# An attention stage that makes the next stage's weight parts in place, with outputs' parts and fetched sums a pair behind

## The reference, cut to what matters

```python
q = _l2norm(q)                      # (B, 16, 1024, 64)
k = _l2norm(k) * key_temp           # (B, 4, 1024, 64), repeated 4 times
scores = jnp.einsum('bhqd,bhkd->bhqk', q, kg) * scale
attn = jax.nn.softmax(jnp.where(causal, scores, min), axis=-1)
out = jnp.einsum('bhqk,bhkd->bhqd', attn, vg)
return out.transpose(0, 2, 1, 3).reshape(B, S, LATENT) @ w_o.T
...
x = x + s * g                       # end of layer 0
xn = _layernorm(x, axis=-1)         # layer 1 begins
q, k, v = xn @ wq.T, xn @ wk.T, xn @ wv.T
low = jnp.einsum('bsd,hrd->bshr', x, A)
```

## Time and profile before

| | us |
|---|---|
| median of three runs | 2434.13 |
| profiled execution, its own time | 2439.68 |
| its span in the profile | 2437.6 |
| attention stage, first exp to last (L2145) | 1048.8 to 1439.4 |
| busy over the whole span: PE, DVE, ACT, POOL | 2036.1, 1523.0, 1127.0, 818.7 |
| mean granted clock of TensorE | 0.928 of 2.4 GHz |

### The profile page before, as it was taken

One profiled execution on the slowest core, in us unless ns is written; L12 is line 12 of the kernel. 1 busy time (PEld: TensorE's weight loads), 2 busy tenths in 40 slices (PEclk: granted clock), 3 DMA queues, 4 the chain that ended last, 5 costly groups with the idle time before them and its releaser, 6 DMA issues. The chain is left out here.

```text
span 2437.6 us, 47417 instructions
## 1 busy us (share of the span) xinstructions
PE 2036.1 (84%) x19400; PEld 995.0 (41%) x19400; DVE 1523.0 (62%) x3033; ACT 1127.0 (46%) x2021; POOL 818.7 (34%) x782
## 2 busy tenths in 40 slices
PE   7999989997578899867878859776488988888878
PEld 3444435554233334533444424333244443444434
DVE  3543354434679998435766663556788888888813
ACT  1221146554323342155655630233277777777760
POOL 0210312122545646222565320224443334334310
PEclk9999999998789999888989979988699999999999
DMA  6020101103222112453312338322664564543424
GB/s 233 35 87 35 67 16 31 31 14 118 78 62 80 50 52 69 142 138 57 105 66 83 118 104 217 101 74 74 131 148 67 70 85 65 74 79 58 68 72 145
DMA packets 162028, 207.08 MB, mean 85 GB/s; under 512 B 58962, under 2 KB 100436, under 8 KB 159124
## 3 DMA queue, kind: packets, MB, share of 16 engines
q1 hardware_dynamic: 158756, 189.83, 31.7%
q10 hardware_dynamic: 3056, 14.23, 1.7%
HBM read 139.75 MB, written 64.25 MB: 84 GB/s over the span
## 5 line engine op out<-in xcount | busy, mean ns | idle before, releaser
L3278 DVE TENSOR_REDUCE f_chunk_max<-f_ps_a 128x64 f32<-128x1024 f32 x320 | 319.4, 1032 | 47.5 <-PE f_ps_a L3022 25.0
L3151 ACT ACTIVATE conv_in<-f_ps_s 128x512 f32<-128x512 f32 x480 | 258.7, 603 | 86.9 <-PE f_ps_s L3053 42.3
L2145 ACT ACTIVATE d_probs<-d_ps_s,d_shift 128x512 f32<-128x512 f32 (+3 forms) x384 | 194.2, 589 | 92.1 <-PE d_ps_s L2061 66.6
L3022 PE MATMUL f_ps_a<-conv_in 128*32 128x512 bf16 (+3 forms) x3072 | 201.4, 340 | 41.1 <-DVE f_chunk_max L3278 24.3
L3053 PE MATMUL f_ps_s<-f_qs,f_ks 128*32 128x512 bf16 x2304 | 209.3, 384 | 23.2 <-ACT f_qs L3142 14.6
L2056 PE MATMUL d_ps_s<-conv_in 128*64 128x512 f16 (+3 forms) x768 | 137.4, 360 | 76.9 <-ACT d_probs L2145 68.0
L1422 PE MATMUL c_ps_c<-conv_in,c_wT 128*128 128x512 f16 x768 | 184.9, 400 | 18.0 <-DVE c_odd L1723 13.6
L3218 POOL TENSOR_SCALAR f_absent<-f_rest 128x576 f32<-128x576 f32 x32 | 54.4, 1699 | 304.1 <-DVE f_rest L3295 180.1
L2072 PE MATMUL d_ps_o<-d_probs,conv_in 128*64 128x512 f32 (+3 forms) x768 | 150.3, 500 | 5.3 <-ACT d_probs L2145 4.4
L3075 PE MATMUL f_ps_o<-conv_in,f_v 128*32 128x512 f32 (+2 forms) x1152 | 125.6, 522 | 27.4 <-ACT conv_in L3151 27.4
L3142 ACT ACTIVATE f_qs<-f_ps_s 32x512 bf16<-32x512 f32 x192 | 112.6, 586 | 75.7 <-PE f_ps_s L3036 73.2
(11 more groups left out here) (379 smaller groups left out, 4539.1 us busy)
## 6 DMA issues: line engine op xcount, KB each, us to landing
conv_in<-qk SPq DMA_DIRECT2D x96, 128.0 KB, 4.1
f_qs<-qk SPq DMA_DIRECT2D x96, 128.0 KB, 4.7
conv_in<-q_parts SPq DMA_DIRECT2D x8, 1024.0 KB, 5.2
o_parts<-d_o_part SPq DMA_DIRECT2D x32, 256.0 KB, 2.3
conv_in<-o_parts SPq DMA_DIRECT2D x8, 1024.0 KB, 8.4
qk<-e_part SPq DMA_DIRECT2D x12, 640.0 KB, 4.9
f_qs<-qk SPq DMA_DIRECT2D x96, 64.0 KB, 4.6
rows<-in_qc_w ACTq DMA_DIRECT2D x3, 1536.0 KB, 7.0
```

Of the source, the lines that this page charges most:

```text
L2145: act.activation(probs[n % RING][SCORES[c][1]][:, lo:hi], ps_s[c % BANKS][:, lo - hi + CH:], ACT.Exp, bias=shift[:, 0:1], scale=HD0 ** -0. ...
L3022: last = pe.matmul(out[side(e), h, 0:w], qa[u][:, 2 * p + h, side(e, qt * P)], ka[u][:, kh * CH:kh * CH + w], start=True, stop=not last_keys)
L3151: act.activation(probs[m % HELD][:, :, at:at + P], bank_of["s", i, n][:].rearrange("p (h n) -> p h n", n=P), ACT.Exp, scale=HD1 ** -0.5).t ...
L3278: dve.tensor_reduce(chunk_max[:, qt - 2, :, at:at + w // CHUNK], src.rearrange("p h (c k) -> p h c k", k=CHUNK), AX.X, ALU.max).then_inc(a ...
```

## The change

Three things in the attention stage change, and with them the layout of the next stage's weights.

1. *Outputs' parts a pair later.* ACT makes `high(p-2)` after kt 2 of pair p, where it made `high(p-1)` after kt 6. DVE makes `low(p-2)` after the third gather, just ahead of `divide(p-1)`, where it stood ahead of `combine(p-1)`. After the last pair ACT makes two of them.
2. *Fetched sums later.* The fetches come after steps 7 and 24 instead of 4 and 19; `sizes` go to pairs 1 and 3, `scales` to pairs 2 and 4 and ahead of the combine, and the pieces to pairs 5 to 12.
3. *Parts in place.* POOL writes the scaled fp32 piece to a small buffer `w_scaled` in `d_w_space`, and both fp16 parts over the piece itself, which has just their size. The stores to `e_parts`, the load back and POOL's waits for the stores are gone. The parts of a piece now lie behind each other in `whole`, so the middle stage addresses them piece by piece.

```diff
-        SPLIT_FROM, SPLIT_EACH = 4, 2
+        SPLIT_FROM, SPLIT_EACH = 5, 2
...
-                if SPLIT_FROM < p <= LAST_SPLIT + 1:
-                    store_pieces(p - 1)
...
-                if p == LAST_SPLIT + 1:
-                    for i in range(2):
-                        sp.wait_ge(split_stored[i], 16 * ((len(PIECES) + 1 - i) // 2))
-                    weights.load_parts(sp)
...
-                if kt == 6 and p > 0:
-                    high(p - 1)
+                if kt == 2 and p > 1:
+                    high(p - 2)
...
-                elif n == 4:
+                elif n == 7:
                     fetch(0, 1, 0)
...
-                elif n == QT + SIZES + 2:
+                elif n == QT + SIZES + 7:
                     fetch(1, SIZES, 1)
             copy(ALL - 1)
+            high(ALL - 2)
             high(ALL - 1)
...
-                to, src = w_parts[x % 2], weights.whole[:, at:at + n]
+                src, whole = w_scaled[x % 2][:, 0:n], weights.whole[:, at:at + n]
+                to = whole.bitcast(FP16).rearrange("p (a c) -> p a c", a=2)
                 pool.wait_ge(scaled, 4)
                 if x >= 2:
-                    pool.wait_ge(split_stored[x % 2], 16 * (x // 2))
-                pool.tensor_scalar(src, src, weights.scale[:, own:own + 1], None, ALU.mult).then_inc(split, 1)
+                    pool.wait_ge(split, 3 * (x - 1))
+                pool.tensor_scalar(src, whole, weights.scale[:, own:own + 1], None, ALU.mult).then_inc(split, 1)
...
-                if p > 1:
-                    low(p - 2)
+                if p in (2, SPLIT_FROM - 1):
+                    scales(*((0, 1, 0) if p == 2 else (1, 4, 1)))
                 if p > 0:
                     combine(p - 1)
                 gather(p, 2)
-                if p == 0:
+                if p > 1:
+                    low(p - 2)
+                if p == 1:
                     sizes(0, 1, 0)
-                elif p == 2:
+                elif p == 3:
                     sizes(1, 4, 1)
...
-        self.oT = [x.rearrange("p (m d) -> p m d", d=D) for x in oT]
+        self.oT = oT.rearrange("p (m a d) -> p a m d", a=2, d=D)
```

More of the change, by code:

```diff
@@ L1931, in attend_phase @@
         root = sb("root", [P, 4])
-        w_parts = [w_space[:].bitcast(FP16)[:, n * 2 * (CH + 16):(n + 1) * 2 * (CH + 16)].rearrange("p (a c) -> p a c", a=2) for n in range(2)]
+        w_scaled = [w_space[:, n * (CH + 16):(n + 1) * (CH + 16)] for n in range(2)]
         temp = sb("temp", [P, 1])
@@ L1963, in attend_phase @@
         split = sem("d_split")
-        split_stored = [sem(f"d_split_stored{i}") for i in range(2)]
         o_high = sem("d_o_high")
@@ L1994, in store @@
                     sp.dma_start(dram["o0_parts"][n, g * (G0 // 2) + i, :, b * S:(b + 1) * S], o_parts[p % 2][n][:]).then_inc(stored[p % 2], 16)
[L1996 to L2000, removed]
             sp.dma_start(v_w[:].rearrange("p (k c) -> p k c", k=KD), dram["w_qkvT"].rearrange("p (k o) -> p k o", k=KD)[:, :, LAT + KVD:LAT + 2 * KVD])\
@@ L2286, in _ @@
                 gather(p, 2)
-                if p == 0:
+                if p > 1:
+                    low(p - 2)
+                if p == 1:
                     sizes(0, 1, 0)
-                elif p == 2:
+                elif p == 3:
                     sizes(1, 4, 1)
-                elif p in (1, SPLIT_FROM - 1):
-                    scales(*((0, 1, 0) if p == 1 else (1, 4, 1)))
                 if p > 0:
@@ L2326, in __init__ @@
         self.ends = [sum(self.WIDTHS[:i]) for i in range(len(self.WIDTHS) + 1)]
-        self.parts = self.whole[:].bitcast(FP16).rearrange("p (a n) -> p a n", a=2)
-        oT, qkT, tokT = [[self.parts[:, part, lo:hi] for part in range(2)] for lo, hi in zip(self.ends, self.ends[1:])]
-        self.oT = [x.rearrange("p (m d) -> p m d", d=D) for x in oT]
-        self.qkT = [x.rearrange("p (i k n) -> p i k n", i=self.NQK, k=KD) for x in qkT]
-        self.tokT = [x.rearrange("p (k t) -> p k t", k=KD) for x in tokT]
+        oT, qkT, tokT = [self.whole[:, lo:hi].bitcast(FP16) for lo, hi in zip(self.ends, self.ends[1:])]
+        self.oT = oT.rearrange("p (m a d) -> p a m d", a=2, d=D)
+        self.qkT = qkT.rearrange("p (i a k n) -> p a i k n", i=self.NQK, a=2, k=KD)
+        self.tokT = tokT.rearrange("p (h a k t) -> p a h k t", h=2, a=2, k=KD // 2)
         self.scale = sb("scale", [P, 4])
@@ L2353, in load @@
         sp.dma_start(self.br[:], dram["lora_br"].rearrange("(a n) -> a n", a=1).to_broadcast((P, HL))).then_inc(self.tables, 16)
-    def load_parts(self, sp):
-        sp.dma_start(self.parts, self.dram["e_parts"]).then_inc(self.w_loaded, 16)
     def load_tokens(self, sp, c):
@@ L2536, in project @@
                 if c == 0:
-                    pe.wait_ge(weights.w_loaded, 32)
+                    pe.wait_ge(weights.w_loaded, 16)
                 pe.wait_ge(loaded[c % 2], 160 * (c // 2 + 1))
@@ L2542, in project @@
                         for i, (w, x) in enumerate(PARTS):
-                            last = pe.matmul(ps_s[t % 2][:], o_in[c % 2][:, x, m, t * P:(t + 1) * P], oT[w][:, m, :],
+                            last = pe.matmul(ps_s[t % 2][:], o_in[c % 2][:, x, m, t * P:(t + 1) * P], oT[:, w, m, :],
                                              start=(m == i == 0), stop=(m == MQ - 1 and i == len(PARTS) - 1))
@@ L2563, in rest @@
                         for i, (w, x) in enumerate(PARTS):
-                            last = pe.matmul(ps_y[t % 2][:, 0:TOK], xT[:, x, k, t * P:(t + 1) * P], tokT[w][:, k, :],
+                            last = pe.matmul(ps_y[t % 2][:, 0:TOK], xT[:, x, k, t * P:(t + 1) * P], tokT[:, w, k // 2, k % 2, :],
                                              start=(k == i == 0), stop=(k == KD - 1 and i == len(PARTS) - 1))
@@ L2570, in rest @@
                         for n, (w, x) in enumerate(PARTS):
-                            last = pe.matmul(ps_q[i % 2][:], qkT[w][:, i, k, :], xT[:, x, k, :],
+                            last = pe.matmul(ps_q[i % 2][:], qkT[:, w, i, k, :], xT[:, x, k, :],
                                              start=(k == n == 0), stop=(k == KD - 1 and n == len(PARTS) - 1))
@@ L3517, in program @@
     scratch("o0_parts", (2, MQ, P, T), FP16)
-    scratch("e_parts", (P, 2, MiddleWeights.COLS), FP16)
     scratch("sizes", (SIZES * P,))
```

6 lines of the change are left out of this document (3 added, 3 removed).

## The result

| | before | after |
|---|---|---|
| median of the runs side by side | 2435.33 us (2433.21 to 2437.3, 4 runs) | 2355.93 us (2351.24 to 2359.68, 4 runs) |
| profiled execution, its span, mean clock | 2439.68, 2437.6, 0.928 | 2359.68, 2357.9, 0.935 |
| first exp of the stage | 1048.82 | 1050.84 |
| first exp to last copy | 391.18 | 300.91 |
| last copy to the next stage's first matmul | 22.65 | 28.51 |

The ratio is 0.9673, 95% interval 0.9653 to 0.9693: faster by 3.3%, against a forecast of 2354.0 us. All of it comes from this stage; what lies before and behind it took 4.7 us more in this execution, which is within what these parts vary by from one execution to the next: over the profiles of all kernels here the first exp comes between 1045.4 and 1057.2, and the stretch behind the stage takes 972.1 to 977.6 us.

The account below looks back on a forecast made before the run. No engine was full: PE's idle time came from ACT waiting on DVE's latency before high. Gains 22.9 + 55.9 + 5.6 - 4.3 = 80.1 us took the median 2434.1 to 2354.0 us; range 2341 to 2380.

Parts of the forecast that it names:

- pairs 0, 1, 2: Start of the stage: later fetches shorten ACT's waits for the sums' DMA; gains 4.4, 4.7 and 13.8 us, together 22.9.
- twelve intervals: Copies up to pair 15: 283.9 us become 228.0, eight pairs with pieces at 19.3, four without at 18.4; gain 55.9.
- last pair: Pair 15 to the last copy: 21.61 us become 16.0 without the stall and the slow stretch; gain 5.6.
- tail: Behind the last copy: the combine waits for high(14) and low(14), shifting all behind it; -4.3 us, perhaps 3 to 6.
- the rest of the program: Next stage: matmuls read the parts with the same contiguous rows, the load was hidden; zero, perhaps -1 to +1 us.
- The half clock: PE in a pair: 3.03 us at half clock go with the stall and become 1.52 at full, giving 18.3 us.
- The parts in place: Pairs 5 to 12: POOL's removed waits cost almost nothing; pieces beside DVE's gathers and combine make a pair 19.3 us.
- The port: Rival, chance 0.12: DVE (except the reciprocal) and POOL exclude each other; pairs with pieces 22.4 us, total 2379.
- rough handing-over: Rival, chance 0.11: PE waits in bits, part of the half clock stays; pairs 19.9, with pieces 20.9, total 2373 us.
- The stall did not move: Answers a rival, chance 0.05: ACT or PE finds another wait on DVE's chain, pairs stay at 23.2, total 2408 us.
- No pair ran at 1.2 GHz: Answers the slower case, chance 0.02: PE working without rest gets 1.2 GHz; all at half clock +155 us, 2590.
- rival 1: Chance 0.12: DVE's 8.5 us and POOL's 13.9 exclude each other on the shared port, 22.4 us a pair with pieces.

Follow-up runs that it names:

- x4_stores_kept: Kernel after with the stores of the pieces and the load of the parts put back; 2413.0 us, ratio 0.9883 to the kernel before.
- x1: Kernel before with only the outputs' parts moved a pair later; 2421.8 us, ratio 0.9921.
- x6_three_pieces: Kernel after with three pieces a pair in pairs 5 to 9 in place of two in 5 to 12; one profiled run, 2382.42 us.
- x11: Kernel after with the stores of the pieces kept but issued ahead of the store of the outputs; 2354.83 us, ratio 0.9659 to the kernel before.
- x3_in_place: Kernel before with only the parts of the weights written in place; 2438.6 us, ratio 0.9983.
- x8_combine_first: Kernel after with the last combine ahead of low(14); one profiled run, 2353.95 us.
- x10_tokens_early: x8_combine_first with the next stage's first loads of g and x issued two pairs earlier; 2349.5 us, ratio 0.963 to the kernel before.

## Why the prediction was right

The forecast's mechanism holds: the stall before `high` was DVE's latency, it went, and PE's work at full clock is what is left. Term by term, gains in us:

| term | forecast | measured |
|---|---|---|
| pairs 0, 1, 2 | 4.4, 4.7, 13.8 | 3.6, 3.6, 14.0 |
| twelve intervals | 55.9 | 63.5 |
| last pair | 5.6 | 5.6 |
| tail | -4.3 | -5.9 |
| the rest of the program | 0 | -4.7 |
| sum | 80.1 | 79.7 |

**The twelve intervals: right mechanism, one term mis-sized.** A pair without pieces was put at 18.4 and took 18.37. A pair with pieces was put at 19.3 and took 18.37: the eight make 7.4 of the 7.6 us of difference. The step that failed is the one from DVE's loss to the length of the pair. The loss itself was right, 2.0 forecast against 17.77 less 15.60 = 2.2. But I took only DVE's wait before the reciprocal, 1.44 us, as room, while DVE busy for 15.6 of 18.37 had 2.8. DVE's quotient and `low` are wanted a pair later now, so the 2.2 us fitted into its 2.8 us of idle time. That is read from busy times; no run takes DVE to its limit. The reading of the earlier trace rows that the scaling loses nothing held for the first of a pair's two pieces only: the second took 2.78 us for 1.57 (1231.12). It cost nothing, since POOL still had 0.3 us.

**The half clock.** I read it as going with the stall. In the kernel after, 220 us without a stall show 1.00; the pairs of 27.1 us in x4_stores_kept, with their stall of 8 us on ACT, show 0.88:

```profile
1246.15:1273.25 27.10, 21.11 (x188) 10.64 (x186) 16.08 (x11) 14.10 (x27) 14.51 (x17) 0.88 0.11 40
```

PE is busy for 21.11 us there with the same 188 matmuls that take 18.37, so the half clock cost 2.7 us beside the stall itself. In the stage's profiles of the two kernels and of x1 to x6 and x11, each fall to 0.50 came while PE stood still or right behind it. The reverse does not hold, as the prediction said: in the kernel before PE stood still from 1176 to 1179 and its mean clock from there to 1201 was 1.00.

**The start.** The first fetch still waited 6.93 us, for its DMA took 13.6 us from issue of the store (12.6 before). Pair 1 took 20.40 for 19.3; PE, not ACT, was busiest there (20.05 us at a mean clock of 0.97, ACT 19.10), and no run takes this apart. The second fetch waited for nothing, as forecast.

**The parts in place.** That POOL's wait cost nothing was right for the kernel before (x3_in_place) and is half the truth: I priced the edit by what it freed before and did not say what the other edit would cost without it. By x4_stores_kept against the kernel after (0.9883 and 0.9673) that is 2.1%, some 51 us. It changed no number, since both edits come together.

**The tail.** The combine starts 4.2 us later relative to the copy (4.82 for 0.61), as forecast. What follows was not the chain alone: `low(14)` also releases SP's loads for the next stage, and relative to the copy these were issued 4.6 us later. The last store was issued 4.0 us later and landed 7.76 us behind its issue for 5.86, which makes 5.9. x8_combine_first shows that the chain I priced was not what set the end, and x10_tokens_early that the loads were.

**The rest.** The agreement of the sums, 80.1 and 79.7, is partly luck. The stage gave 4.3 us more than forecast and the rest of the program took 4.7 more, of which the runs show that they vary from one execution to the next: the stretch behind the stage took 974.95 in the kernel before, and 977.64 and 974.93 in two executions of the kernel after. The new places of the parts in the weights cost nothing that can be seen there. Three sums in the prediction are slightly off: the ends of the twelve intervals are 44 and 65 (45 and 64 stand there), 21.61 less 4.26 and 1.5 is 15.85 (16.0), and the combine comes 4.2 us later by its own terms (4.3). None moves the forecast by more than 0.2 us.

**The rivals.** The port (22.4 us a pair) and rough handing-over (19.9) fall with 18.37. The stall did not move: ACT waits at its write of the parts nowhere but behind the last pair. No pair ran at 1.2 GHz: the mean clock was 0.91 and 0.97 in pairs 0 and 1, where PE had waited on the fetch of the sums, and 1.00 from there on.

## What to carry to other kernels

A wait that costs nothing is covered by another one; when that goes, price it anew, by the whole ring of who waits for whom, the queue of DMA issues and the buffers between engines included. When a program-ordered queue holds two stores, put the one whose input is ready first ahead: here one moved line was worth as much as taking the memory out. When a consumer is moved a pair behind, look at its producer's whole idle time as room for new work (2.2 of 2.8 us on DVE here), and count how full each engine is then: POOL was full to 0.3 us.

## What the runs showed of the hardware

DVE and POOL slowed each other beside one another, and did not exclude each other throughout. The fifteen pieces were busy for 52.8 us on POOL before and 75.3 after (scaling 23.5 to 32.1, cast 10.0 to 14.0, subtract 19.3 to 29.2), with DVE's combine at 2.51 for 1.55. In pairs of 18.37 us ran work that, summed as if one excluded the other, is 22.4 (rival 1, an estimate from durations seen without the lengthening). The Trainium skill, "SBUF — State Buffer", section "SBUF: two separate sides", has the loser block fully. The runs agree in that operations of either engine can lengthen, by up to 1.2 us, and differ in the sum, by 4.0 us a pair here and 3.7 in x6_three_pieces (25.7 for 22.0).

A store's landing depended on what was issued ahead of it: the same two DMAs of 256 KB landed 3.5 us behind their issue with the loads out of the way (x10_tokens_early) and 9.95 us behind it with them (x8_combine_first).
